# A cache-attention kernel on one core: four key units without a cache task, the last four value-cache conversions later, and the second batch's page loads two per unit

## The reference, cut to what matters

```python
x = x + einsum('bct,bcd->bdt', x, L0_weights[subjects])
q, k, v = x @ Wq.T, x @ Wk.T, x @ Wv.T             # per head
q, k = rope(rmsnorm(q) * qw, pos), rope(rmsnorm(k) * kw, pos)
k_all = concat([k_cache[block_table], k]); v_all = concat([v_cache[block_table], v])
scores = where(valid, q @ k_all.T * SCALE, -1e30)
x = x + (softmax(scores) @ v_all) @ Wo.T
```

## Time and profile before

| | |
|---|---|
| median of 3 runs | 1012.82 us (1011.83 to 1014.14) |
| the profiled execution | 1012.16 us, span 1010.1 us |
| busy share: TensorE, VectorE, ScalarE, GpSimd | 96%, 81%, 73%, 54% |
| TensorE's granted clock, mean | 0.997 |
| chain that ended last, by engine | PE 70%, DVE 15%, ACT 5%, issue 5%, DMA 3%, POOL 2% |

### The profile page before, as it was taken

How to read it: one execution, slowest core, us unless ns; L and a number is a source line. 1 busy time by engine, 2 the same in 40 slices (tenths; PEclk the granted TensorE clock), 3 DMA queues, 4 the chain that set the end, 5 groups by cost and what they waited for, 6 DMA issues and landing times.

```text
span 1010.1 us, 24830 instructions
## 1 busy us (share of the span) xinstructions
PE 966.2 (96%) x8123; PEld 803.1 (80%) x8123; DVE 819.5 (81%) x1749; ACT 735.7 (73%) x2008; POOL 546.2 (54%) x715
## 2 busy tenths in 40 slices
PE   6899999999899999899999999999999999989998
PEld 4678888887677787688888888888888888878885
DVE  7789999999997689888877877777887787777770
ACT  5798999988774688777767767776776676766660
POOL 6565665565893068646644555454445545544540
PEclk9899999999999999999999999999999999999999
DMA  5799999989998989999999998998999998999940
GB/s 197 279 298 309 352 385 370 385 279 389 387 324 280 363 297 368 340 239 267 286 316 255 284 308 279 288 286 287 311 252 289 318 287 246 312 289 277 264 124 11
DMA packets 249903, 294.89 MB, mean 292 GB/s; under 512 B 79024, under 2 KB 206512, under 8 KB 247216
## 3 DMA queue, kind: packets, MB, share of 16 engines
q1 hardware_dynamic: 231088, 226.07, 74.9%
q0 software_dynamic: 18688, 67.25, 17.8%
HBM read 231.77 MB, written 46.27 MB: 275 GB/s over the span
## 4 chain that ended last, share of the span: by engine, by line
PE 70%; DVE 15%; ACT 5%; issue 5%; DMA 3%; POOL 2%; SPq 0%; DVEq 0%; ACTq 0%; POOLq 0%
PE ps_y L1491 16%; PE ps_proj L1491 15%; PE ps_o L1566 13%; PE ps_s L1529 8%; PE ps_s L1533 7%; PE ps_t L1540 7%; PE ps_rt L1661 2%; DMA w_nat<-in_L_cond_Wq 2%; DVE c_stage L1387 2%; DVE rot L1363 2%; DVE probs L1230 2%; DVE stage L1373 1%; PE ps_t L1548 1%; DVE rot L1355 1%; PE ps_o L1578 1%
## 5 line engine op out<-in xcount | busy, mean ns | idle before, releaser
L934 POOL TENSOR_SCALAR probs<-probs,recip 128x544 f32<-128x544 f32 (+1 forms) x256 | 162.7, 635 | 288.2 <-DVE recip L1238 280.5
L1008 ACT ACTIVATE probs<-probs,neg_max 128x544 f32<-128x544 f32 x256 | 191.0, 746 | 147.2 <-DVE neg_max L1230 143.9
L1230 DVE CUSTOM_DVE_ANT_0 probs<-ps_s,mask,row_scale 128x544 f32<-128x544 f32 x256 | 200.4, 783 | 64.2 <-PE ps_s L1533 60.9
L1566 PE MATMUL ps_o<-pt,vs 128*128 128x128 f16 x3072 | 213.5, 220 | 0.6 <-DMA vs<-v_pages,v_row 0.6
L1566 PEld LDWEIGHTS ps_o<-pt,vs 128*128 128x128 f16 x3072 | 192.7, 98 | 15.2 <-DMA vs<-v_pages,v_row 1.2
L887 POOL TENSOR_TENSOR roped<-rot 128x256 f32<-128x256 f32 x160 | 144.4, 923 | 82.6 <-DVE rot L1355 74.4
L1250 DVE SCALAR_TENSOR_TENSOR pt<-ps_t,pt 128x512 f16<-128x512 f32 x190 | 129.9, 684 | 48.9 <-ACT pt L1014 47.9
L1491 PE MATMUL ps_proj<-wt_hi,x0t_hi 128*128 128x512 f32 x384 | 159.7, 417 | 6.3 <-DVE x0t_lo L1188 5.8
L1491 PE MATMUL ps_y<-wo,ot_hi 128*128 128x512 f16 x512 | 153.6, 382 | 2.5 <-DVE ot_lo L1262 2.5
L1491 PE MATMUL ps_proj<-wt_hi,x0t_lo 128*128 128x512 f32 x384 | 151.4, 395 | 0.0
L1491 PE MATMUL ps_proj<-wt_lo,x0t_hi 128*128 128x512 f32 x384 | 150.6, 393 | 0.0
(11 more groups left out here) (156 smaller groups left out, 1657.0 us busy)
## 6 DMA issues: line engine op xcount, KB each, us to landing
kt<-k_pages_t SPq DMA_DIRECT2D x512, 128.0 KB
c_nat<-in_L_cond_k_cache SPq DMA_DIRECT2D x32, 512.0 KB, 6.2
q_t<-stage SPq DMA_DIRECT2D x64, 256.0 KB, 7.5
c_nat<-in_L_cond_v_cache SPq DMA_DIRECT2D x32, 512.0 KB, 7.0
qt<-q_t SPq DMA_DIRECT2D x32, 512.0 KB, 3.3
w_nat<-in_L_cond_Wq SPq DMA_DIRECT2D x8, 1024.0 KB, 8.7
k_pages_t<-c_stage SPq DMA_DIRECT2D x16, 512.0 KB, 5.6
c_nat<-in_L_cond_Wo SPq DMA_DIRECT2D x16, 512.0 KB, 7.5
```

Of the source, the lines that this page charges most:

```text
L934: pool.tensor_scalar(part, part, col(recip, i), 1.0, ALU.mult, ALU.mult).then_inc(p_norm, 1)
L1008: act.activation(pr, pr, ACT.Exp, bias=col(neg_max, i), scale=-1.0, accum_out=col(row_sum, i)).then_inc(a_exp, 1)
L1230: dve.tensor_tensor_reduce(out=probs_of(i), in0=ps_s[:, score_cols(i):score_cols(i) + KEYS], in1=mask[(i // HK) % 2][:, mask_at(i):mask_at ...
L1566: ins = pe.matmul(ps_o[n % 2][:, jl * P:(jl + 1) * P], v[:, part, :], pt[pt_slot(i)][:, NCH * half + c, :], start=jl == 1 and c == 0 and k ...
```

## The change

Four key units (66, 69, 72, 75) get no cache task. The last four value conversions leave the interleaved list and stand at its end, so they fall on units 79 to 82; the tasks from 58 on change order and units accordingly, the last scan stays in unit 78. The second batch's pages are loaded two per unit from unit 85 to 92 instead of one per unit from 80 to 95, and the wait for all conversions moves with them from unit 80 to 85.

```diff
-    KEYS_AT, NEXT_KEYS_AT, PREFETCH, NEW_V_AT = 54, 80, 87, 93
+    KEYS_AT, NEXT_KEYS_AT, PREFETCH, NEW_V_AT = 54, 85, 87, 93
...
-             + [("scan", n) for n in WO_SCANS[:7]] + mixed(V_CONVS, WO_SCANS[7:]))
+             + [("scan", n) for n in WO_SCANS[:7]] + mixed(V_CONVS[:-4], WO_SCANS[7:])
+             + [("conv", n) for n in V_CONVS[-4:]])
...
+    TASK_FREE = (66, 69, 72, 75)
+    TASK_UNITS = [TASK_AT + t // 2 for t in range(2 * PAIRS)] + [
+        u for u in range(TASK_AT + PAIRS, NU) if u not in TASK_FREE]
     for t in range(len(TASKS)):
-        TASK_IN[TASK_AT + t // 2 if t < 2 * PAIRS else TASK_AT + t - PAIRS].append(t)
+        TASK_IN[TASK_UNITS[t]].append(t)
...
                 if u == NEXT_KEYS_AT:
                     converted(sp, NCONV)
-                if NEXT_KEYS_AT <= u < NEXT_KEYS_AT + NPP:
-                    load_pages(1, u - NEXT_KEYS_AT, 1)
+                if NEXT_KEYS_AT <= u < NEXT_KEYS_AT + NPP // 2:
+                    load_pages(1, 2 * (u - NEXT_KEYS_AT), 2)
```

## The result

| | before | after |
|---|---|---|
| median of 6 runs | 1012.86 us | 1016.57 us |
| lowest to highest | 1011.27 to 1014.14 | 1015.34 to 1017.64 |
| profiled execution, its span | 1012.16, 1010.1 | 1015.68, 1013.7 |

The ratio after to before is 1.0037, with a 95% interval of 1.0024 to 1.0050: 3.7 us slower. The prediction, 1010.9 with a range of 1008.9 to 1015.2, missed on both counts. Ratios and intervals leave out one execution of a later kernel (no free unit), which took 1407.48 us at a granted clock of 0.66; without it that kernel's median is 1009.50 instead of 1009.72.

A forecast was written before the change was run, and what follows sets the result against it. VectorE was taken to bound the key units, unlike phase 1's other stages, bound by TensorE. TensorE -2.2 and late weights +0.3 gave -1.9 us against the median of 1012.82: 1010.9, range 1008.9 to 1015.2.

The forecast's parts named there:

- What bounds the kernel: Phase 1: VectorE, busy 55.29 of 56 us, bounds the key units; TensorE loses 8.8 us there.
- Part 1: Four free key units: three conversions fewer in units 64 to 77 bring unit 80's transposes 4.9 us sooner, at 300.5.
- Part 2: Conversions in units 79 to 82: VectorE reaches unit 83 when it did before, so TensorE keeps 2.2 of 4.9 us.
- the idle behind the square root: Unit 81: VectorE idles some 1.5 us in place of 0.87, behind ScalarE's table load, root and conversion.
- the drain of 1.38 us: ScalarE's table switch in unit 81: a drain left out of the forecast; with it the gain would be 0.8 us.
- TensorE stop of 2.7 us at units 85 and 86: Value units: TensorE, 4.9 us ahead, stops about 2.7 us for VectorE's unit 83 write.
- the forecast's 2.2: Lead in us that TensorE keeps after its stop at units 85 and 86.
- Part 3: DMA queues: unit 88's weight load leaves at 335 to 336; late weights cost 0 to +2.0 us, taken as +0.3.
- the time of the gathers: First batch's value gathers start at about 325 instead of 308.52, taking 5.6 us of all DMA engines; counted as free.
- the time of an issue: SyncE in units 85 to 88: issuing two pages per unit takes an estimated 1.2 us.
- Rival 3: Slower: gathers take their 5.6 us in front of queries and weights; +2 to +5 us, centre 1015.5, chance 0.18.
- its test: Sign of rival 3: ScalarE or TensorE waits over 2 us for a DMA (weights, queries, new values) in 341 to 356.

The follow-up runs named there:

- no free unit: Changed kernel without its four free units, last four conversions in a row in units 75 to 78: 1009.72 us, ratio 0.9978.
- two free units: Changed kernel with two free units (66 and 72) in place of four, last conversion in unit 80: 1010.53 us, ratio 0.9982.
- Tasks alone: Changed kernel with the second batch's pages one per unit in units 83 to 92, then two per unit: 1016.01 us, ratio 1.0044.
- gathers behind the weights: Changed kernel with GpSimd waiting, ahead of the four gathers, until unit 88's weight load has landed: 1015.2 us, ratio 1.0040.
- weights first (both): Changed kernel, pages from unit 88: weights in units 84, 85, 87, 91 (1014.12 us), or in 84, 85, 86, 91 with second queries in 91 (1015.16).
- both remedies: Changed kernel with weights in units 84, 85, 87, 91, pages from unit 88, and 18 more TensorE products in unit 94: 1014.96 us, ratio 1.0036.
- both kernels without gathers: Kernel before and changed kernel, each with zeros written in place of the first batch's four gathers: 1009.47 us (0.9970) and 1009.69 us (0.9981).
- gathers late: Kernel before with the first batch's four gathers started only when TensorE has finished unit 85: 1012.8 us, ratio 1.0014.
- products in the wait: Changed kernel with 18 additional 128x128 matmuls in TensorE's idle time in unit 94: 1014.92 us, ratio 1.0030.
- weights ahead of pages: Changed kernel with weight loads in units 84, 85, 87, 91 and the second batch's pages in units 88 to 95: 1014.12 us, ratio 1.0022.

## Why the prediction was wrong, by its steps

**What bounds the kernel**: right. VectorE was the bound of the key units, and relief there moved TensorE.

**Part 1**, 4.9 us: right in number, in part by luck. Measured 4.87 us, once the two executions are aligned at unit 63. Taken raw the rows say 6.56. Unit 80's transposes came at 298.86, forecast 300.5; add the 1.68 of head start and it is 300.54. But the prediction's count (1.48 us for each conversion fewer in units 64 to 77, plus 0.5) can be tried on the two kernels between. No free unit has nine conversions there, as before, so 0.5 us; it gains 1.9 at unit 80 (61.96 against 63.88 us from unit 63). Two free units have seven, so 3.5; they gain 2.4. The agreement within 0.1 at four is closer than the count is good for. Nor is the earlier trace rows split as the prediction says: three of its 14 conversions start 0.43 to 0.44 us after GpSimd's additions and still take only 1.37 to 1.38.

**Part 2**, VectorE reaches unit 83 when it did before: mostly right after alignment. Its write came at 314.67 against 317.47, of which 1.68 is the head start; the true 1.1 us is more than the forecast's 0.4 at best. The term that was too large is the idle behind the square root, put at 1.5. VectorE in the kernel after, where it adds, waits and converts:

```profile
304.65 0.41 DVE L1447 TENSOR_TENSOR row_part<-row_part,w_eps 128x256 f32<-128x256 f32 x1
...
306.58 1.28 DVE L1391 SCALAR_TENSOR_TENSOR c_stage<-c_nat,scale,c_stage 128x1024 f16<-128x1024 f32 x1 [0.27 <-ACT c_stage L1116]
```

The idle was 0.27, because ScalarE loads its table before the sum that the root waits for is ready:

```profile
303.50 1.28 ACT L1099 ACT_TABLE_LOAD   x1
305.09 0.42 ACT L1099 ACTIVATE squares<-row_part 128x256 f32<-128x256 f32 x1 [0.31 <-DVE row_part L1447]
305.41 1.14 ACT L1116 ACTIVATE c_stage<-c_nat,scale 128x1024 f16<-128x1024 f32 x1
```

So the table load isn't behind the sum, and the drain of 1.38 us that the Trainium skill gives ("ScalarE: Activation LUTs", What ACT_TABLE_LOAD costs) isn't seen between these rows; leaving it out was right. The TensorE stop of 2.7 us at units 85 and 86 that the forecast took off the lead isn't in this form in the trace: its one wait for VectorE there is 0.86 us (near 312), and at the first copy of unit 89, 328.01, a lead of 4.85 us (3.2 aligned) is still there, 1.7 less than at the last transposes. More lead than the forecast's 2.2, then, not less.

**Part 3**, weights +0.3: this is the step that failed. ScalarE waited 7.2 us for weights, and the first exponential came 3.2 us late (aligned) where the sum had the kernel 1.9 ahead. It failed in three places.

First, only one weight load was followed, unit 88's. The one before it was the first to come late: it landed 11.7 us after its issue and ScalarE lost 3.38 us on it. Its margin in the kernel before was some 5 us (issued at 326.43, landed 6.9 later, copied at 338.30). It left 1.4 us sooner, landed 4.8 us slower, and would have been wanted at 333.4, 4.9 us sooner: 5.0 + 1.4 - 4.8 - 4.9 is -3.3, the wait that ScalarE shows.

Second, the time of the gathers. The forecast set them at 325, with the last conversion stored at 318 and landed by 324 to 326. It was stored at 314.77, landed in 2.6 us where the forecast had 6 to 8, and the first gather was issued at 318.37. The prediction then argued that gathers which leave the slack stretch make it slacker. True (share 0.25 at 311 to 314 where the earlier trace rows has 0.78), and worthless: SyncE, which issues in order, stood 5.2 us waiting for the last conversion there and issued nothing that could use the slack.

Third, the prediction took the time of an issue as fixed (1.2 us for two pages). Behind the gathers SyncE's issues themselves were longer, by some 3 us up to the third weight load, which left at 337.29, 339.0 once aligned, not 335 to 336. Its latency of 8.5 us is near the 8.1 of the earlier trace rows; the loss is in when it left.

**Rival 3** is what happened, at 0.18. It gave 1015.5; the result is 1016.57, and its test ("a wait for a DMA over 2 us in 341 to 356") came out at 3.83 us at 345.85. That the gathers in front make the weights late is shown by three runs: their late start alone makes a landing of 11.4 us in the kernel before, without them the loads of the changed kernel land in 5.6 to 7.3, and with two free units, gathers at 313.78 instead of 318.37 and less lead, no wait is left. That this lateness is the whole loss isn't shown. Their absence takes 5.7 us off the changed kernel and 3.0 off the other, but removes their traffic as well as their place; moving only their place, behind the third weight load, left the ratio at 1.0040. That traffic of two queues shares the DMA engines, as the Trainium skill has it ("DMA: Bandwidth & Descriptors", Queues, rings and completion order), fits the landing times; packet by packet is more than these rows can show.

**What the prediction had no term for** is TensorE's clock. The idle of 5.08 us was followed by the lower level, 1.39 us lost in one unit (4.16 - 2.77), which was absorbed by the first product with the output weights; the fall near 905 us (8 x 0.21, 1.7 us) was not.

The record has the mean granted clock of every run, and it goes with the time. The changed kernel's six runs have 0.9937 in the mean, the kernel before's three groups 0.9967 to 0.9972. Over 1014 us that is 3.0 to 3.6 us of full clock (an estimate), about the whole loss. Tasks alone, gathers behind the weights, weights first (both) and both remedies, all slower than the kernel before, have 0.9935 to 0.9957; no free unit, two free units and both kernels without gathers, all faster, 0.9970 to 0.9984; gathers late, in between in time, has 0.9969. But the clock alone isn't the loss either: with products in the wait the mean is back at 0.9972 and the median is still 1014.92.

**What stays open.** Of the 3.7 us in the medians, 2.7 are tied to the gathers by removing them, with an uncertainty almost as large; how they and the rest divide between late weights, the lead that weights and keys could not follow, and the clock is not shown. Why the fall near 905 us comes in some kernels (the changed one, tasks alone, gathers late, weights first) and not in others with the same wait of some 2.4 us (before, no free unit, products in the wait) isn't settled, nor is what the clock adds to the median. Filling the idle time with products gave 1014.92 against 1016.57, within the intervals. No version was tried in which weights, new values and gathers are all moved for the four free units.

## What to carry to other kernels

Before work is moved past a point that releases DMAs, list every transfer that will then be in flight together, with the margin of each user, not only the user that looks tightest; lead won upstream shrinks all these margins at once. A freed slot is worth what the next deadline leaves of it: here none or two free units beat the kernel before, and four lost to it. An engine that issues in order can itself be slowed by the traffic, so a wait that a chain of waits puts down to one DMA is worth checking against that DMA's landing. And align two traces at a place ahead of the edit before subtracting rows; 1.7 of 6.6 us were not the edit's.

## What the runs showed that was not expected

- The same load of 1024 KB landed in 5.6 to 7.3 us in the changed kernel without gathers (5.9 to 9.0 in the kernel before without them) and in 6.3 to 8.3 in the kernel before. Issued as the second load 2.6 to 6.7 us after the first gather, it needed 11.4 to 13.8. A first load issued 0.9 to 1.4 us after the first gather still landed in 7.0 to 8.2.
- Issuing can take long too: SyncE's issue of a load or store, 0.3 to 0.8 us in this stretch of the kernel before, took 2.06, 1.98, 4.68 and 6.47 us behind the gathers.
- An idle time of 5.08 us of TensorE was followed by 3 to 4 us at 1.2 GHz; with 18 small products in it the clock stayed at 1.00. The length of the idle time alone doesn't decide: 2.35 us was followed by the lower level in the changed kernel without gathers (0.50 from 344 us on), 3.02 us was not with weights ahead of pages.
- One early fall of the clock (26 to 36 us) varied between executions: no fall in two of the profiled ones, a loss of 1.7 us in most, and one of 3.4 us in three (the kernel before among them), nearly what this change moved the time.
